# A decoder layer's last token tile: work rows and banks of its own, its merge in four parts, its steps reordered

## Chip, cores and metric

One core of one Trainium2 chip. The metric is the device time of one execution of the whole kernel in microseconds, median of several runs. All arithmetic on the path discussed here is float32, apart from the bf16 operands of the quantized matmuls.

## The reference, cut to what matters

Eight sequences of 128 tokens with 256 features go through three blocks, each followed by a residual addition and a layer norm: a selective state-space scan, a cross attention with 16 heads over 128 context rows, and a feed-forward block with Hadamard transforms and quantization. The change touches the end of the second block and the third:

```
x = layernorm(x + scan_block(x))
x = layernorm(x + attention(x, ctx))          # per head: probabilities, context, latent
                                              # ... then ctx @ Wo.T over all heads: the "merge"
h = hbitlinear(x, w_up)                       # fwht(x), 8-bit rounding by the row maximum, matmul
h = square(relu(h))
h = hbitlinear(h, w_down)                     # fwht over 512 columns, rounding, matmul
x = layernorm(x + h)
```

## The kernel before, in words

The scan block runs first (up to some 260 us). Then the attention and the feed-forward block run together, by tiles of 128 tokens: T = 8 tiles, numbered 0 to 7 (T - 2 is tile 6, T - 1 is tile 7). Heads are handled in G = 4 groups of four. A software pipeline written out by hand in `slots`, one version for each engine, interleaves three tiles: projection and attention of tile t, merge and the first steps of tile t - 1, the later steps of tile t - 2. Each engine has its own program, in fixed order, and waits on semaphores that count up by tile or by group; an instruction queued behind a waiting one waits too. Behind the loop stands an epilogue, also by hand, for what is left of tiles 6 and 7 (lines 740 to 755 for TensorE, 1010 to 1022 for ScalarE, 1126 and 1127 for GpSimd, 1427 to 1440 for VectorE).

The functions for one tile:

- `turn_prob`, `context` (TensorE, lines 623 to 642): transposes ("turns") of a group's probabilities into bank 7, and the context matmuls; ScalarE evicts with `take_prob` and `take_ctx` (lines 948 to 958), the latter counts `cte`.
- `merge_heads` (TensorE, line 647): eight accumulating matmuls 128x128 by 128x256, two for each head group, into bank 7 (`merged`). It waits for the evictions of all four groups. A float32 matmul of this size is two records in the trace.
- `norm2` (VectorE, line 1327): residual, layer norm statistics, the power on GpSimd (line 1064), the normalized row, and the two halves of the first Hadamard level (lines 1340 and 1341).
- `ffn(t, step)`: step 5 turns these halves (TensorE) and evicts them (ScalarE); 6 is the Hadamard matmul, then `quantize` of 256 columns on VectorE (lines 1347 to 1358); 7 turns the rounded row; 8 multiplies with the up weights, ScalarE does relu and square (lines 977 and 979); 9 does two Hadamard levels on VectorE (lines 1366 to 1370), turns on TensorE (line 680) and evicts; 10 is the Hadamard matmul and `quantize` of 512 columns; 11 turns (line 690) and evicts (line 982); 12 multiplies with the down weights and adds the residual (line 1382). `norm3` is the last layer norm, then comes a store of the tile.

All steps of all tiles work in one PSUM bank, 6 (`tail`), and in one set of work rows in SBUF (`x2T`, `qf`, `hr`, `hT`, `qb16`, `qT16`, `xh`). That is why step 5 of a tile waits for step 12 of the one ahead:

```python
if step == 5:
    pe.wait_ge(xh_s, t + 1)
    need(pe, ln3, 4 * t - 3)
```

All plain matmuls go through the helper at line 410; turns stand on lines of their own (532, 565, 629, 659, 669, 680, 690). In the epilogue TensorE's order before is: context of group 2, turn of the last group, step 9 of tile 6, context of the last group, step 10 of tile 6, the merge of tile 7, steps 11 and 12 of tile 6, steps 5 to 12 of tile 7. VectorE's is: normalize of the last group, steps 9 and 10 of tile 6, norm2 of tile 7, step 12 and norm3 of tile 6, steps 6, 9, 10, 12 and norm3 of tile 7.

The rope of the attention multiplies in PSUM banks 0 and 1 and writes `pc` and `psn` (1536 words a partition each), which are not used any more once the last group's sum is made, at 487.9 us.

Of the kernel before, what the change touches and what calls it, by code (L numbers as in the profile page):

```python
# [19 lines left out]
BF16 = mybir.dt.bfloat16  # L20
# [4 lines left out]
P = 128  # L25
T = 8
DM = 256
# [4 lines left out]
NH = 16  # L32
# [3 lines left out]
FF = 512  # L36
TOK = T * P
KM = DM // P
# [10 lines left out]
G = 4  # L49
# [15 lines left out]
def need(eng, sem, count):  # L65

    if isinstance(count, int) and count <= 0:
        return
    eng.wait_ge(sem, count)


def decoder_layer(nc, x_fm, x_tiles, wx, wz, conv_w, w_xp, w_dt, b_dt, a_log, d_skip, w_out,
                  w_q, w_kcq, w_qr, w_kr, w_kckv, w_o, ctx_kv, w_up, w_dn,
                  ident_c, rope_q, rope_kv, had, out, zs_dram, ud_dram, x1_dram, a_dram):
    with ExitStack() as stack:
# [6 lines left out]
        ps = stack.enter_context(nc.psum_tensor("ps", [P, 8, 512], F32))  # L82
# [5 lines left out]
        Pw = sb("Pw", [P, NH // 2, DM])  # L88
# [103 lines left out]
        x2T = carve(256).rearrange("p (k n) -> p k n", k=KM)  # L192
# [85 lines left out]
        scores_of = ps[:, 4:6, 0:256].rearrange("p e (i n) -> p e i n", i=2)  # L278
        latent_of = ps[:, 2:4, 0:P]
        context_of = ps[:, 3, 256:512]  # L280
        turned, merged = ps[:, 7, :], ps[:, 7, 0:DM]

        block = stack.enter_context(nc.Block())

# [123 lines left out]
        def _(pe):  # L408
# [232 lines left out]
                                  probT[:, g % 2, 2 * i + e, :])  # L641
                last.then_inc(cxm, 1)

            tail = ps[:, 6, :]
            tail16 = tail.bitcast(BF16)

            def merge_heads(t):
                pe.wait_ge(cte, G * t + G)
                need(pe, ln2, 4 * t - 3)
                for i in range(NH // 2):  # L650
                    last = mm(merged, ctxT[:, i, :], Pw[:, i, :], i == 0, i == NH // 2 - 1)
                last.then_inc(om, 1)

            def ffn(t, step):
                if step == 5:
                    pe.wait_ge(xh_s, t + 1)
                    need(pe, ln3, 4 * t - 3)
                    for k in range(KM):
                        last = pe.transpose(tail[:, k * P:(k + 1) * P], xh[:, k * P:(k + 1) * P], ident[:, :])
                    last.then_inc(t5m, 1)  # L660
                elif step == 6:
                    pe.wait_ge(t5e, t + 1)
                    for k in range(KM):
                        last = mm(tail[:, k * P:(k + 1) * P], x2T[:, k, :], had_s)
                    last.then_inc(t6m, 1)
                elif step == 7:
                    pe.wait_ge(q1_s, t + 1)
                    for k in range(KM):
                        last = pe.transpose(tail16[:, k * P:(k + 1) * P], qb16[:, k * P:(k + 1) * P],
                                            identb[:, :])  # L670
                    last.then_inc(t7m, 1)
                elif step == 8:
                    pe.wait_ge(t7e, t + 1)
                    for k in range(KM):
                        last = mm(tail, qT16[:, k, :], wupq[:, k, :], k == 0, k == KM - 1)
                    last.then_inc(t8m, 1)
                elif step == 9:
                    pe.wait_ge(lev2_s, t + 1)
                    for k in range(FF // P):
                        last = pe.transpose(tail[:, k * P:(k + 1) * P], hr[:, k * P:(k + 1) * P], ident[:, :])  # L680
                    last.then_inc(t9m, 1)
                elif step == 10:
                    pe.wait_ge(t9e, t + 1)
                    for k in range(FF // P):
                        last = mm(tail[:, k * P:(k + 1) * P], hT[:, k, :], had_s)
                    last.then_inc(t10m, 1)
                elif step == 11:
                    pe.wait_ge(q2_s, t + 1)
                    for k in range(FF // P):
                        last = pe.transpose(tail16[:, k * P:(k + 1) * P], qb16[:, k * P:(k + 1) * P],  # L690
                                            identb[:, :])
                    last.then_inc(t11m, 1)
                elif step == 12:
                    pe.wait_ge(t11e, t + 1)
                    for k in range(FF // P):
                        last = mm(tail[:, 0:DM], qT16[:, k, :], wdnq[:, k, :], k == 0, k == FF // P - 1)
                    last.then_inc(t12m, 1)
# [46 lines left out]
            scores(last, T - 1, G - 1)  # L744
            ffn(T - 2, 8)
            context(last - 1, T - 1, G - 2)
            turn_prob(last, T - 1, G - 1)
            ffn(T - 2, 9)
            context(last, T - 1, G - 1)
            ffn(T - 2, 10)  # L750
            merge_heads(T - 1)
            ffn(T - 2, 11)
            ffn(T - 2, 12)
            for step in range(5, 13):
                ffn(T - 1, step)


# [1 line left out]
        def _(act):  # L759
# [197 lines left out]
                act.activation(ctxT[:, 2 * g:2 * g + 2, :].rearrange("p i n -> p (i n)"), context_of,  # L957
                               ACT.Copy).then_inc(cte, 1)

            tail = ps[:, 6, :]  # L960
            tail16 = tail.bitcast(BF16)

            def ffn(t, step):
                if step == 5:
                    act.wait_ge(t5m, t + 1)
                    act.activation(x2T.rearrange("p k n -> p (k n)"), tail[:, 0:256], ACT.Copy).then_inc(t5e, 1)
                elif step == 9:
                    act.wait_ge(t9m, t + 1)
                    act.activation(hT.rearrange("p k n -> p (k n)"), tail, ACT.Copy).then_inc(t9e, 1)
                elif step == 7:  # L970
                    act.wait_ge(t7m, t + 1)
                    act.activation(qT16[:, 0:KM, :].rearrange("p k n -> p (k n)"), tail16[:, 0:256],
                                   ACT.Copy).then_inc(t7e, 1)
                elif step == 8:
                    act.wait_ge(t8m, t + 1)
                    act.wait_ge(deq_s, 2 * t + 1)
                    act.activation(hr, tail, ACT.Relu, scale=deq).then_inc(relu_s, 1)
                    act.wait_ge(relu_s, t + 1)
                    act.activation(hr, hr, ACT.Square).then_inc(sq_s, 1)
                elif step == 11:  # L980
                    act.wait_ge(t11m, t + 1)
                    act.activation(qT16.rearrange("p k n -> p (k n)"), tail16[:, 0:512], ACT.Copy).then_inc(t11e, 1)
# [34 lines left out]
            take_prob(last, G - 1)  # L1017
            ffn(T - 2, 9)
            take_ctx(last, T - 1, G - 1)
            ffn(T - 2, 11)  # L1020
            for step in (5, 7, 8, 9, 11):
                ffn(T - 1, step)


# [106 lines left out]
        def _(dve):  # L1131
# [190 lines left out]
                dve.tensor_tensor(prob[:, g % 2], prob[:, g % 2], rsum.unsqueeze(2).to_broadcast([P, HG, P]),  # L1322
                                  ALU.mult).then_inc(nrm, 1)

            tail = ps[:, 6, :]

            def norm2(t):
                dve.wait_ge(st_x1, 16 * (t + 1))
                dve.wait_ge(om, t + 1)
                need(dve, x3_s, t - 1)  # L1330
                dve.tensor_tensor(xpre2, merged, x1r, ALU.add).then_inc(ln2, 1)
                dve.wait_ge(ln2, 4 * t + 1)
                center(ln2, 4 * t + 1, xpre2, stats2, aggr2, veps2)
                dve.wait_ge(rs2, t + 1)
                need(dve, xr_s, t)
                dve.tensor_scalar(x2_new, xpre2, aggr2[:, 0:1], rstd2, ALU.subtract, ALU.mult).then_inc(x2_s, 1)

                dve.wait_ge(x2_s, t + 1)
                need(dve, t5m, t)
                dve.tensor_tensor(xh[:, 0:P], x2_new[:, 0:P], x2_new[:, P:DM], ALU.add)  # L1340
                dve.tensor_tensor(xh[:, P:DM], x2_new[:, 0:P], x2_new[:, P:DM], ALU.subtract).then_inc(xh_s, 1)

            def quantize(t, n, src, m, inv, de, w, chain, done):


                root = float(np.sqrt(n))
                dve.tensor_reduce(m, src, AX.X, ALU.max, apply_absolute_value=True).then_inc(chain, 1)
                dve.wait_ge(chain, 5 * t + 1)
                dve.tensor_scalar(m, m, Q_EPS * root, 1.0 / QB, ALU.max, ALU.mult).then_inc(chain, 1)
                dve.wait_ge(chain, 5 * t + 2)  # L1350
                dve.reciprocal(inv, m).then_inc(chain, 1)
                dve.tensor_scalar(de, m, 1.0 / root, w, ALU.mult, ALU.mult).then_inc(deq_s, 1)
                dve.wait_ge(chain, 5 * t + 3)
                dve.tensor_scalar(qf[:, 0:n], src, inv, -QB, ALU.mult, ALU.max).then_inc(chain, 1)
                dve.wait_ge(chain, 5 * t + 4)
                dve.tensor_scalar(qf[:, 0:n], qf[:, 0:n], QB, ROUND, ALU.min, ALU.add).then_inc(chain, 1)
                dve.wait_ge(chain, 5 * t + 5)
                dve.tensor_scalar(qb16[:, 0:n], qf[:, 0:n], -ROUND, None, ALU.add).then_inc(done, 1)

            def ffn(t, step, normed=None):  # L1360
                if step == 9:

                    dve.wait_ge(sq_s, t + 1)
# [65 lines left out]
            row_max(last, G - 1)  # L1429
            normalize(last, G - 1)  # L1430
            ffn(T - 2, 9)
            ffn(T - 2, 10)
            norm2(T - 1)
            ffn(T - 2, 12, T)
            norm3(T - 2)
            ffn(T - 1, 6)
            ffn(T - 1, 9)
            ffn(T - 1, 10)
            ffn(T - 1, 12, T)
# [85 lines left out]
```

## Time and profile before

| what | value |
|---|---|
| median of 3 runs | 531.21 us |
| lowest, highest | 529.97, 535.25 us |
| time of the profiled execution | 533.35 us |
| its span | 531.5 us |
| outside the span | 1.85 us |
| mean granted TensorE clock | 0.915 |
| TensorE busy | 430.6 us (81%) |
| VectorE busy | 404.7 us (76%) |
| ScalarE busy | 311.5 us (59%) |
| GpSimd busy | 217.2 us (41%) |

The busy shares are means over stages with different limits, so what a change at the end is worth is read from the last 45 us alone. The granted clock is given as a share of full speed: 1.00 is the level of 2.4 GHz, 0.50 that of 1.2 GHz. Names in the rows are those of the memory regions: `ps` is PSUM, `reg_a` and `reg_b` the large work regions in SBUF (`had_s` lies in `reg_a`, the work rows in `reg_b`), `Pw` the merge's weights, `wupq` and `wdnq` the quantized weights.

### The profile page before, as it was taken

What the parts mean: (1) busy time and instruction counts of PE and PEld (TensorE: products, weight loads), DVE (VectorE), ACT (ScalarE), POOL (GpSimd) and SP (SyncE); (2) the same over time, 40 slices, a digit from 0 to 9 for tenths busy, and PEclk for the clock granted to TensorE, in tenths of its full rate; (3) what the DMA queues carried; (4) which work ended last, traced back from release to release, by engine and by line L of the source; (5) the groups of instructions that cost most, each with busy time, mean ns of one, the idle gap of its engine ahead of it and who ended that gap; (6) DMA issues with size and microseconds to landing.
All of it is one profiled execution on the core that took longest, in us unless ns stands there. A gap on an engine that the chain in (4) does not pass through costs nothing.

```text
span 531.5 us, 10547 instructions
## 1 busy us (share of the span) xinstructions
PE 430.6 (81%) x3616; PEld 345.8 (65%) x3616; DVE 404.7 (76%) x742; ACT 311.5 (59%) x722; POOL 217.2 (41%) x157
## 2 busy tenths in 40 slices
PE   4979923838777586777999999999999999998733
PEld 1435623527667475666888888888888888887512
DVE  1967699978999969996575687877778777876453
ACT  3666996959999969985143444535255453525320
POOL 2300009985987949780323232323233232322010
PEclk9999975978899879967999999999999999999765
DMA  8942633053011511103000000000000000000000
GB/s 295 389 205 81 195 93 108 20 120 110 21 41 30 145 54 51 39 21 123 22 1 2 11 2 22 0 0 20 0 20 0 20 0 0 20 0 20 1 10 10
DMA packets 18652, 30.85 MB, mean 58 GB/s; under 512 B 2112, under 2 KB 11712, under 8 KB 17920
## 3 DMA queue, kind: packets, MB, share of 16 engines
q1 hardware_dynamic: 18624, 30.49, 17.4%
q8 instruction: 16, 0.26, 0.2%
q14 instruction: 12, 0.10, 0.1%
HBM read 24.16 MB, written 6.32 MB: 57 GB/s over the span
## 4 chain that ended last, share of the span: by engine, by line
PE 40%; issue 19%; DVE 19%; ACT 9%; POOL 8%; DMA 3%; SPq 1%; DVEq 1%; POOLq 0%; ACTq 0%
PE ps L410 33%; POOL reg_b L1059 5%; PE ps L532 3%; DVE reg_b L1256 3%; PE ps L629 2%; ACT hc L854 2%; DMA ud_t<-ud_dram 2%; POOL reg_b L1082 2%; DVE ps L1249 2%; DVE ps L1246 2%; DVE reg_b L1309 1%; ACT reg_b L944 1%; ACT ps L846 1%; DVE reg_b L1194 1%; POOL small L1064 1%
## 5 line engine op out<-in xcount | busy, mean ns | idle before, releaser
L1059 POOL TENSOR_TENSOR reg_b<-reg_c,reg_a 128x1024 f32<-128x1024 f32 x56 | 130.4, 2369 | 58.8 <-DVE reg_c L1199 58.6
L1082 POOL TENSOR_TENSOR reg_b<-reg_b 128x768 f32<-128x768 f32 x32 | 58.0, 1811 | 134.5 <-DVE reg_b L1309 107.3
L410 PE MATMUL ps<-x1T,Mw 128*128 (+1 forms) x768 | 95.2, 281 | 0.0
L410 PEld LDWEIGHTS ps<-x1T,Mw 128*128 128x128 f32 x768 | 89.9, 195 | 4.4 <-issue 3.9
L854 ACT ACTIVATE hc<-reg_b,bc 128x512 f32<-128x512 f32 x112 | 80.4, 718 | 20.9 <-PE ps L532 14.7
L532 PE MATMUL ps<-ident,hc 128*128 128x128 f32 x452 | 73.0, 309 | 19.7 <-ACT hc L854 19.3
L1256 DVE SCALAR_TENSOR_TENSOR reg_b<-reg_c,bc,ps 128x512 f32<-128x512 f32 x112 | 81.8, 736 | 0.0
L532 PEld LDWEIGHTS ps<-ident,hc 128*128 128x128 f32 x452 | 58.9, 160 | 30.5 <-ACT hc L854 29.3
L1249 DVE TENSOR_TENSOR ps<-ps,reg_b 128x512 f32<-128x512 f32 x96 | 65.7, 690 | 8.9 <-ACT ps L846 8.8
L846 ACT ACTIVATE ps<-reg_b 128x512 f32<-128x512 f32 x112 | 66.2, 592 | 4.1 <-POOL reg_b L1059 4.1
L944 ACT ACTIVATE reg_b<-ps,small 128x128 f32<-128x128 f32 x128 | 45.1, 367 | 24.5 <-DVE small L1314 24.5
L1064 POOL TENSOR_TENSOR small<-small 128x1 f32<-128x1 f32 x24 | 13.2, 551 | 102.0 <-DVE small L1274 102.0
L938 ACT ACTIVATE reg_b<-ps 128x256 f32<-128x256 f32 x32 | 12.3, 384 | 53.6 <-PE ps L410 53.6
L410 PE MATMUL ps<-reg_b 64*128 64x128 f32 (+1 forms) x512 | 42.6, 294 | 0.7 <-ACT reg_b L938 0.5
L410 PE MATMUL ps<-reg_b,Nw 64*64 64x128 f32 (+1 forms) x768 | 42.0, 287 | 1.2 <-POOL reg_b L1082 1.2
L532 PE MATMUL ps<-ident,ud_t 128*128 128x128 f32 x32 | 7.5, 377 | 39.6 <-DVE yT L1264 17.8
L410 PEld LDWEIGHTS ps<-reg_b,Nw 64*64 64x64 f32 (+1 forms) x768 | 30.4, 150 | 12.7 <-issue 11.6
L410 PEld LDWEIGHTS ps<-reg_b 64*128 64x128 f32 (+1 forms) x512 | 30.4, 162 | 11.4 <-issue 2.6
L410 PE MATMUL ps<-xw,Nw 128*128 128x512 f32 x64 | 29.7, 622 | 7.3 <-DMA xw<-x_fm 7.3
L1308 DVE TENSOR_TENSOR reg_b<-ps,reg_a 128x768 f32<-128x768 f32 x32 | 30.4, 951 | 4.9 <-PE ps L410 4.6
L532 PEld LDWEIGHTS ps<-ident,ud_t 128*128 128x128 f32 x32 | 4.8, 188 | 41.9 <-issue 21.6
L1309 DVE TENSOR_TENSOR reg_b<-ps,reg_a 128x768 f32<-128x768 f32 x32 | 30.3, 947 | 0.0
(143 smaller groups left out, 709.9 us busy)
## 6 DMA issues: line engine op xcount, KB each, us to landing
reg_a<-a_dram SPq DMA_DIRECT2D x4, 1024.0 KB, 7.3
Mw<-w_o SPq DMA_DIRECT2D x1, 2048.0 KB, 15.3
ud_dram<-reg_b SPq DMA_DIRECT2D x4, 512.0 KB, 4.4
zs_dram<-x1T SPq DMA_DIRECT2D x4, 512.0 KB, 3.7
ud_t<-ud_dram SPq DMA_DIRECT2D x8, 256.0 KB, 3.1
zs_t<-zs_dram SPq DMA_DIRECT2D x8, 256.0 KB, 2.6
xw<-x_fm SPq DMA_DIRECT2D x2, 512.0 KB, 6.1
mring<-w_q SPq DMA_DIRECT2D x4, 256.0 KB, 4.1
```

What stands on the lines that cost most here:

```text
L410: return pe.matmul(o, l, r, start=start, stop=stop)
L532: return pe.matmul(o, src, ident[:, :], start=start, stop=stop, is_transpose=True, skip_group_check=True)
L846: act.activation(ps[:, n % RING, :], dA[:, n // SA % RING, n % SA, :], ACT.Exp, scale=-1.0).then_inc(da_s, 1)
L854: act.activation(hc[:, (n + 1) % WRING, :], H[:, n, :], ACT.Copy, scale=bc[:, t, s:s + 1]).then_inc(hc_s, 1)
L944: last = act.activation(prob[:, g % 2, h, :], scores_of[:, h % 2, h // 2, :], ACT.Exp, bias=negm[:, g % 2, h:h + 1], accum_out=sums[:, g % ...
L1059: pool.tensor_tensor(dA[:, g % RING], delta_r[:, bass.ds(t, 1), :].to_broadcast([P, SA, DI]), Abc[:, g * SA:(g + 1) * SA, :], ALU.mult).th ...
L1064: pool.tensor_tensor(r, v, neghalf, ALU.pow).then_inc(o, 1)
L1082: pool.tensor_tensor(rq[:, g % 2].rearrange("p a c n -> p (a c n)"), pc[:, g % 2].rearrange("p a c n -> p (a c n)"), psn[:, g % 2].rearran ...
L1249: dve.tensor_tensor(E_n, E_n, H[:, n, :], ALU.mult).then_inc(dah_s, 1)
L1256: dve.scalar_tensor_tensor(H[:, n, :], step_du(t), step_b(t, n), ps[:, n % RING, :], ALU.mult, ALU.add).then_inc(h_s, 1)
L1308: dve.tensor_tensor(pc[:, g % 2], v, ropeq_s[:, 0], ALU.mult)
L1309: dve.tensor_tensor(psn[:, g % 2, ::-1], v, ropeq_s[:, 1], ALU.mult).then_inc(ropem, 1)
```

## The change

The last tile gets its own PSUM banks (0 for the steps, 1 for the merge) and its own work rows, laid over `pc` and `psn`. Its merge is issued as four groups of two matmuls, each behind the eviction of its head group; the first waits also until the last rope has read bank 1. Step 5 of the last tile no longer waits for `ln3` of tile 6. In the epilogue TensorE issues steps 5 and 6 of tile 7 ahead of steps 11 and 12 of tile 6, ScalarE evicts step 5 of tile 7 ahead of step 11 of tile 6, and VectorE does norm2 of tile 7 ahead of step 10's quantize of tile 6, and step 6's quantize of tile 7 ahead of step 12 and norm3 of tile 6. GpSimd's and the DMA queue's programs stay.

```diff
-        turned, merged = ps[:, 7, :], ps[:, 7, 0:DM]
+        turned = ps[:, 7, :]
+        rope_words = pc.rearrange("p b a c n -> p (b a c n)"), psn.rearrange("p b a c n -> p (b a c n)")
+        loop_work = (ps[:, 6, :], ps[:, 7, 0:DM], x2T, qf, hr, hT, qb16, qT16, xh)
+        last_work = (ps[:, 0, :], ps[:, 1, 0:DM], rope_words[0][:, 0:256].rearrange("p (k n) -> p k n", k=KM),
...
+                     rope_words[1][:, 1024:1280])
+
+        def work_of(t):
+
+            return last_work if isinstance(t, int) and t == T - 1 else loop_work
...
+            def merge_group(t, g):
+
+                merged = work_of(t)[1]
+                pe.wait_ge(cte, G * t + g + 1)
+                for i in (2 * g, 2 * g + 1):
+                    last = mm(merged, ctxT[:, i, :], Pw[:, i, :], i == 0, i == NH // 2 - 1)
+                if g == G - 1:
+                    last.then_inc(om, 1)
...
                 if step == 5:
                     pe.wait_ge(xh_s, t + 1)
-                    need(pe, ln3, 4 * t - 3)
+                    if not (isinstance(t, int) and t == T - 1):
+                        need(pe, ln3, 4 * t - 3)
...
             context(last - 1, T - 1, G - 2)
+            pe.wait_ge(ropem, G * T)
+            merge_group(T - 1, 0)
+            merge_group(T - 1, 1)
             turn_prob(last, T - 1, G - 1)
             ffn(T - 2, 9)
+            merge_group(T - 1, 2)
             context(last, T - 1, G - 1)
             ffn(T - 2, 10)
-            merge_heads(T - 1)
+            merge_group(T - 1, 3)
+            ffn(T - 1, 5)
+            ffn(T - 1, 6)
             ffn(T - 2, 11)
             ffn(T - 2, 12)
-            for step in range(5, 13):
+            for step in range(7, 13):
                 ffn(T - 1, step)
...
             take_ctx(last, T - 1, G - 1)
+            ffn(T - 1, 5)
             ffn(T - 2, 11)
-            for step in (5, 7, 8, 9, 11):
+            for step in (7, 8, 9, 11):
                 ffn(T - 1, step)
...
             ffn(T - 2, 9)
+            norm2(T - 1)
             ffn(T - 2, 10)
-            norm2(T - 1)
+            ffn(T - 1, 6)
             ffn(T - 2, 12, T)
             norm3(T - 2)
-            ffn(T - 1, 6)
             ffn(T - 1, 9)
```

## Rows read from the trace of the kernel before

**Rows 1.** The page: the chain's shares by engine, and the granted clock in 40 slices

```profile
PE 40%; issue 19%; DVE 19%; ACT 9%; POOL 8%; DMA 3%; SPq 1%; DVEq 1%; POOLq 0%; ACTq 0%
...
PEclk9999975978899879967999999999999999999765
```

**Rows 2.** The chain that ended last, 485 to 532 us: start us, us, what

```profile
497.66 7.33 PE ps L410 x32
```

**Rows 3.** Timeline 485 to 532 us: start us, us, engine, line, operation, tiles [idle before]

```profile
494.65 0.66 PE L629 MATMUL ps<-ident,reg_b 128*128 128x128 f32 x4 [2.15 <-DVE reg_b L1322]
...
496.54 1.12 PE L680 MATMUL ps<-ident,reg_b 128*128 128x128 f32 x4 [1.23 <-DVE reg_b L1370]
...
497.59 1.12 PE L410 MATMUL ps<-reg_b 128*64 128x128 f32 x8
...
498.64 2.08 PE L410 MATMUL ps<-reg_a,reg_b 128*128 128x128 f32 x8
...
500.51 4.46 PE L410 MATMUL ps<-Pw,reg_b 128*128 128x256 f32 x16
500.75 0.69 DVE L1347 TENSOR_REDUCE small<-ps 128x1 f32<-128x512 f32 x1 [4.27 <-PE ps L410]
...
503.11 0.43 DVE L1358 TENSOR_SCALAR reg_b<-reg_b 128x512 bf16<-128x512 f32 x1
...
505.06 0.42 DVE L1331 TENSOR_TENSOR reg_b<-ps,reg_b 128x256 f32<-128x256 f32 x1 [1.52 <-PE ps L410]
...
507.78 0.28 DVE L1341 TENSOR_TENSOR reg_b<-reg_a 128x128 f32<-128x128 f32 x1
...
510.75 0.42 DVE L1347 TENSOR_REDUCE small<-ps 128x1 f32<-128x256 f32 x1 [0.19 <-PE ps L410]
...
512.44 0.29 DVE L1358 TENSOR_SCALAR reg_b<-reg_b 128x256 bf16<-128x256 f32 x1
...
512.79 0.40 PE L669 MATMUL ps<-identb,reg_b 128*128 128x128 bf16 x2 [2.08 <-DVE reg_b L1358]
...
516.12 0.42 DVE L1366 TENSOR_TENSOR reg_b<-reg_b 128x256 f32<-128x256 f32 x1 [3.38 <-ACT reg_b L979]
...
524.48 0.61 PE L690 MATMUL ps<-identb,reg_b 128*128 128x128 bf16 x4 [2.88 <-DVE reg_b L1358]
525.13 0.60 ACT L982 ACTIVATE reg_b<-ps 128x512 bf16<-128x512 bf16 x1 [5.65 <-PE ps L690]
...
525.78 1.04 PE L410 MATMUL ps<-wdnq,reg_b 128*128 128x256 bf16 x4 [0.69 <-ACT reg_b L982]
```

**Rows 4.** Stretches: sum, busy of PE, PEld, DVE, ACT, POOL, granted clock, DMA

```profile
495.00:496.00 1.00, 0.31 (x3) 0.07 (x1) 0.97 (x3) 0.77 (x2) 0.00 (x0) 0.69 0.00 0
...
502.00:503.00 1.00, 1.00 (x5) 0.83 (x5) 0.97 (x2) 0.00 (x0) 0.00 (x0) 0.90 0.00 0
...
509.00:510.00 1.00, 0.53 (x3) 0.51 (x3) 0.34 (x2) 0.38 (x1) 0.48 (x1) 0.52 0.00 0
```

**Rows 5.** TensorE's timeline one tile earlier, where the granted clock is 1.00

```profile
465.99 0.66 PE L680 MATMUL ps<-ident,reg_b 128*128 128x128 f32 x4
...
468.31 1.06 PE L410 MATMUL ps<-reg_a,reg_b 128*128 128x128 f32 x8
469.30 1.30 PE L410 MATMUL ps<-reg_b 64*128 64x128 f32 x16
...
473.31 3.62 PE L410 MATMUL ps<-Pw,reg_b 128*128 128x256 f32 x16
```

**Rows 6.** The scan: TensorE's timeline, and stretches of line 410 alone (busy, granted clock)

```profile
209.88 0.66 PE L532 MATMUL ps<-ident,ud_t 128*128 128x128 f32 x4 [2.94 <-DVE yT L1264]
...
205.20:208.70 3.50, 1.06 (x8) 1.00 0.00 0
...
222.30:225.70 3.40, 0.00 (x0) 1.00 0.34 96
...
225.70:229.10 3.40, 0.00 (x0) 0.50 0.02 5
```

More of the change, by code:

```diff
@@ L280, in decoder_layer @@
         context_of = ps[:, 3, 256:512]
-        turned, merged = ps[:, 7, :], ps[:, 7, 0:DM]
+        turned = ps[:, 7, :]
+        rope_words = pc.rearrange("p b a c n -> p (b a c n)"), psn.rearrange("p b a c n -> p (b a c n)")
+        loop_work = (ps[:, 6, :], ps[:, 7, 0:DM], x2T, qf, hr, hT, qb16, qT16, xh)
+        last_work = (ps[:, 0, :], ps[:, 1, 0:DM], rope_words[0][:, 0:256].rearrange("p (k n) -> p k n", k=KM),
+                     rope_words[0][:, 256:768], rope_words[0][:, 768:1280],
+                     rope_words[1][:, 0:512].rearrange("p (k n) -> p k n", k=FF // P),
+                     rope_words[1][:, 512:768].bitcast(BF16),
+                     rope_words[1][:, 768:1024].bitcast(BF16).rearrange("p (k n) -> p k n", k=FF // P),
+                     rope_words[1][:, 1024:1280])
+        def work_of(t):
+            return last_work if isinstance(t, int) and t == T - 1 else loop_work
         block = stack.enter_context(nc.Block())
@@ L642, in context @@
                 last.then_inc(cxm, 1)
-            tail = ps[:, 6, :]
-            tail16 = tail.bitcast(BF16)
             def merge_heads(t):
+                merged = work_of(t)[1]
                 pe.wait_ge(cte, G * t + G)
@@ L652, in merge_heads @@
                 last.then_inc(om, 1)
+            def merge_group(t, g):
+                merged = work_of(t)[1]
+                pe.wait_ge(cte, G * t + g + 1)
[3 more added lines that the diff above has]
+                    last.then_inc(om, 1)
             def ffn(t, step):
+                tail, _, x2T, _, hr, hT, qb16, qT16, xh = work_of(t)
+                tail16 = tail.bitcast(BF16)
                 if step == 5:
                     pe.wait_ge(xh_s, t + 1)
-                    need(pe, ln3, 4 * t - 3)
+                    if not (isinstance(t, int) and t == T - 1):
+                        need(pe, ln3, 4 * t - 3)
                     for k in range(KM):
@@ L958, in take_ctx @@
                                ACT.Copy).then_inc(cte, 1)
-            tail = ps[:, 6, :]
-            tail16 = tail.bitcast(BF16)
             def ffn(t, step):
+                tail, _, x2T, _, hr, hT, _, qT16, _ = work_of(t)
+                tail16 = tail.bitcast(BF16)
                 if step == 5:
@@ L1323, in normalize @@
                                   ALU.mult).then_inc(nrm, 1)
-            tail = ps[:, 6, :]
             def norm2(t):
+                merged, xh = work_of(t)[1], work_of(t)[8]
                 dve.wait_ge(st_x1, 16 * (t + 1))
@@ L1343, in quantize @@
             def quantize(t, n, src, m, inv, de, w, chain, done):
+                qf, qb16 = work_of(t)[3], work_of(t)[6]
                 root = float(np.sqrt(n))
@@ L1360, in ffn @@
             def ffn(t, step, normed=None):
+                tail, _, _, qf, hr, _, _, _, _ = work_of(t)
                 if step == 9:
```

## The prediction

> **What bounds the kernel now.** I read the page first, for how much of the kernel is in reach. The chain is 40% TensorE, and the granted clock falls only in the early slices and in the last two or three [rows 1]. The change touches the last 45 us, so I went to the chain of waits of that stretch. Around 500 us it is TensorE alone, 7.33 us of matmuls without a break, up to 504.99 [rows 2]. What those are stands in the timeline: behind step 9 of tile 6 (496.54) come the context of the last head group, step 10 of tile 6, and the whole merge of tile 7, 4.46 us, which ends at 504.97 [rows 3]. Only then does tile 7's second half begin: 505.06 norm2, 508.06 its halves are ready, 510.75 its first quantization, 512.73 done, 512.79 TensorE's step 7; from there to the end of the span (531.5) it is one serial chain of 18.7 us in which engines take turns. So what counts is when step 7 of tile 7 can start.
>
> Two more things are to be seen. TensorE stood idle for 2.15 us, 492.50 to 494.65, waiting for the probabilities of the last group, and again 1.23 us before step 9 [rows 3]. And the clock: granted 1.00 until about 495.3, then 0.50 (the 1.2 GHz level) until about 502.1, full (2.4 GHz) again, and half from 509 to the end [rows 4]. What fell in the low stretch cost nearly double: step 9 took 1.12 us where the same group takes 0.66 a tile earlier, step 10 2.08 against 1.06, and the merge 4.46 against 3.62 [rows 3, 5].
>
> **The change, part by part.**
>
> *Merge in four parts.* The eight matmuls are the same. Parts 0 and 1 need only head groups 0 and 1, long evicted, and bank 1, free since the last rope read. They stand right after the context of group 2, where TensorE idles. At full clock a matmul of the merge takes 3.62/8 = 0.45 us [rows 5], four take 1.81 us, and the hole is 2.15 us: they end at about 494.3, the turn of the probabilities starts at 494.65 as before. Cost nothing; the cover is the wait for VectorE's normalize, and without it (half clock, 0.89 us each) four take 3.6 us and the turn would be 1.4 us late.
>
> *Part 2* (two matmuls, 0.91 us) is queued behind step 9 and ahead of the last context; *part 3* behind step 10. Behind part 3 waits norm2.
>
> *The clock in that stretch.* Filling the hole leaves TensorE pauses of 0.35 and about 1.3 us between 492 and 497 instead of 2.15 and 1.23. Does the clock still fall? A row on each side: ahead of 209.88 TensorE was idle for 2.94 us, after a stretch with 1.06 us of true matmuls, at 1.00; but in 222.3 to 225.7 there were only turns, with shorter pauses, and the next stretch is at 0.50 [rows 6]. With 1.8 us of matmuls put into the hole I take it as held. The Trainium skill has a rule that speaks against it ("TensorE: Matmul & The Clock Gate", Part 4, PE-mode transpose): a transpose does not count as TensorE activity the way a matmul does. The fall behind 222.3 to 225.7 agrees. By that rule 494.3 to 497.2, with nothing but turns and pauses in it, can still bring a fall; that is rival A below.
>
> *Sum to the end of the merge, clock held.* From 496.54 (step 9's start is set by VectorE, unchanged): step 9 0.66, part 2 0.91, context half of the group of 16 (1.30/2 = 0.65), step 10 1.06, part 3 0.91: 4.19 us [rows 5]. Groups overlap at a join (468.31 + 1.06 = 469.37, the next starts at 469.30), so I take off 0.07 twice: 4.05, merge done at 500.59 instead of 504.97. That is 4.38 us earlier: 1.8 from the two parts moved ahead, 2.6 from the clock. The evictions that step 10 and part 3 wait for (0.6 us for 512 columns, as the one at 525.13 [rows 3], less for the context's 256) lie beside part 2 with the context, and beside step 10.
>
> *VectorE's order.* Before, quantize of tile 6 (500.75 to 503.54, 2.79 us) ran while TensorE merged: it was free. Now norm2 stands ahead of it and waits for part 3, so VectorE idles from 496.5 to 500.6 and the 2.79 us stand on the path. In exchange step 12 and norm3 of tile 6, which filled 508.06 to 510.75 ahead of tile 7's quantize, go behind it. Chain: 500.59 + 0.09 to norm2, 3.00 for it (505.06 to 508.06), 503.68; 0.03 + 2.79 for tile 6's quantize, 506.50; 0.03 + 1.98 for tile 7's (510.75 to 512.73), 508.51 [rows 3]. Steps 5 and 6 of tile 7 on TensorE and the eviction between them fitted into those 2.69 us before, part of them at half clock; now they run beside tile 6's quantize (2.79 us), in a bank of their own and without the wait for ln3, and cost nothing. If they didn't fit, it would be by 0.1.
>
> *What is queued on TensorE.* Steps 11 and 12 of tile 6 now stand between step 6 and step 7 of tile 7. They start with tile 6's quantize: 506.50 + 0.05, step 11 0.61, 0.04, eviction 0.60, 0.04, step 12 1.04, at half clock: 508.88 [rows 3]. That is 0.3 us later than tile 7's quantize, and holds step 7 up by so much. (At full clock these two would be up to 0.8 us shorter, half of 1.65, and hidden.) Which level? Before, TensorE's thin stretch from 505 brought half clock by 509 [rows 4]; the new thin stretch starts at 500.6, so I take half. Step 7 of tile 7 then starts at 508.88 instead of 512.79: 3.9 us earlier. Step 12 and norm3 of tile 6 on VectorE end by about 511.5, before tile 7's step 9 can start (3.3 us behind its step 7, as 516.12 stands to 512.79 [rows 3]: 512.2), so they are hidden; so is the store of tile 6, and GpSimd's copy of x2, which is needed only at the last step.
>
> *Own work rows.* Same sizes, same types, the rope buffers' space: 0. Unknown is the price of the added waits (the three on cte and one on ropem, all met long before): between 0 and 0.2 us on TensorE, of which the chain's issue pieces of 0.02 to 0.04 suggest the lower; I take 0. The loop body has the same instructions; 0.
>
> **Sum:** 4.38 - 2.82 (quantize onto the path) + 2.66 (step 12 and norm3 of tile 6, with their gaps, off it: 508.06 to 510.75 is 2.69, less 0.03) - 0.31 (steps 11 and 12) = 3.9 us. The span of this execution goes from 531.5 to 527.6, its own time from 533.35 to 529.45. That execution lies 2.1 us above the median of the runs; against the median of 531.21 the forecast is 527.3.
>
> **Rivals.**
>
> *A: the clock falls all the same (or later, from about 497).* For it: the rule above, and that the place of the fall need not be the same in every execution. Against: the 2.94 us pause that it survived. If everything from 496.54 runs at half clock: 1.12 for step 9, 2 x 0.9 = 1.8 each for parts 2 and 3, 1.05 and 1.87 between the starts of context, step 10 and merge [rows 3], 7.6 us, merge done at 504.2; then 5.9 us to tile 6's quantize and 2.4 us to step 7, 512.5: a gain of only 0.3. With the clock low for about half of it, 2.2. Middle 1.3, 529.9.
>
> *B: more than that.* If the denser TensorE keeps full clock through tile 7's own steps 7 to 12, each is shorter by what the two levels differ by: 9 by 0.46 and 10 by 1.02 [rows 3, 5], 11 and 12 by at most half of their 1.65, 7 and 8, an estimate from these, by 0.5: 2.8 us, and steps 11 and 12 of tile 6 hide too: gain up to 7.0, 524.2. Against: half clock from 509 to the end in the trace before, with the same pauses. For steps 7 and 8 alone, with 0.3 from steps 11 and 12: 4.7, 526.5.
>
> *C: nothing.* The time saved before step 7 comes back, because something else is late (a transfer, x2's copy, the output). Nothing in the profile is near: 531.2.
>
> *D: slower.* The mechanism is VectorE's new order: tile 6's quantize hangs behind part 3. Its point is merge done at 504.5 (512.79 - 2.4 - 5.9): later than that, and the kernel loses. That takes a clock that is low already at 492.4, so that parts 0 and 1 take 3.6 us, hold up the last turn by 1.4, and nothing rises after: context done 492.4, parts 0 and 1 3.6 (496.0), turn and step 9 2.1, then 1.8, 1.05, 1.87 and 1.8 as in A, 504.7: 0.2 slower, and with the waits' upper bound 0.4: 531.6. Against: 1.00 in all rows up to 495.
>
> **How the numbers follow.** Forecast 0.60, A 0.23, B 0.08, C 0.05, D 0.04. About 1% (5.3 us) is what a measurement of this kernel can tell from no change; three runs spread over 5.3 us. The forecast, 0.7%, is inside, and reaches beyond by the runs' spread about 1 time in 6 (0.10); with most of B 0.15 for faster. Slower by over 1% has only that spread behind C and D: 0.02. Within: 0.83. The range takes most of B below (524.9) and A's and part of C's above (530.6), with 0.2 us of waits and the median's own uncertainty in it.
>
> **What would show it.** Right: TensorE busy with Pw matmuls from 492.4 to 494.3; granted clock 1.00 at 496 to 500; L680-like group of 0.66 us at 496.5; merge done near 500.6; norm2 at once; VectorE in the order norm2, quantize of 512, quantize of 256, then tile 6's last step; step 7 of tile 7 near 508.9 behind the wdnq matmuls. Wrong: half clock at 497 to 501 (A); the last turn of probabilities later than 494.7 (D); step 7 long after both of its predecessors; tile 7's steps 9 and 10 at 0.66 and 1.06 (B).

## The result, and the profile after

| | kernel before | changed kernel |
|---|---|---|
| median of 16 runs | 532.5 us | 529.44 us |
| profiled execution, its span | 533.35, 531.5 us | 528.5, 526.7 us |
| mean granted TensorE clock | 0.915 | 0.922 |

The ratio of the two is 0.993, with a 95% interval of 0.9907 to 0.9953: the changed kernel is about 3.7 us faster (the two medians differ by 3.1). One of the 16 runs of the kernel before took 718.59 us and is left out of the ratio as slow; without it the median before is 532.27 us. The forecast was 3.9.

The two profiles can be laid on each other step by step. I measure from the start of step 9's turns of tile 6 (before 496.54, after 495.90). First TensorE's timeline of the changed kernel, 484 to 512 us (columns as in [rows 3]; what was line 410 is line 422 now, 629 is 641, 659 is 681, 669 is 691, 680 is 702, 690 is 712; on VectorE 1331 is 1358, 1347 is 1375, 1358 is 1386, 1382 is 1411):

```profile
488.65 0.93 PE L641 MATMUL ps<-ident,reg_b 128*128 128x128 f32 x4 [0.50 <-DVE reg_b L1350]
...
491.63 0.96 PE L422 MATMUL ps<-reg_b 128*64 128x128 f32 x8
492.52 1.99 PE L422 MATMUL ps<-Pw,reg_b 128*128 128x256 f32 x8
494.35 0.60 PE L641 MATMUL ps<-ident,reg_b 128*128 128x128 f32 x4
495.90 0.66 PE L702 MATMUL ps<-ident,reg_b 128*128 128x128 f32 x4 [0.94 <-DVE reg_b L1399]
496.39 1.03 PE L422 MATMUL ps<-Pw,reg_b 128*128 128x256 f32 x4
497.35 0.66 PE L422 MATMUL ps<-reg_b 128*64 128x128 f32 x8
497.94 1.16 PE L422 MATMUL ps<-reg_a,reg_b 128*128 128x128 f32 x8
498.93 1.03 PE L422 MATMUL ps<-Pw,reg_b 128*128 128x256 f32 x4
503.11 0.69 PE L681 MATMUL ps<-ident,reg_b 128*128 128x128 f32 x2 [3.15 <-DVE reg_b L1368]
...
505.81 0.61 PE L712 MATMUL ps<-identb,reg_b 128*128 128x128 bf16 x4 [0.31 <-DVE reg_b L1386]
507.11 1.03 PE L422 MATMUL ps<-wdnq,reg_b 128*128 128x256 bf16 x4 [0.69 <-ACT reg_b L1009]
507.94 0.42 PE L691 MATMUL ps<-identb,reg_b 128*128 128x128 bf16 x2
```

The Pw matmuls stand in three places: eight records where the pause of 2.15 us was, four behind step 9, four behind step 10, end at 499.96. Step 9 takes 0.66 us and step 10 1.16 (the next group starts 0.99 behind it, as in [rows 5]), where [rows 3] had 1.12 and 2.08. From step 9 to the end of the merge it is 4.06 us, before 8.43. Steps 11 and 12 of tile 6 (lines 712 and the wdnq matmuls) stand right ahead of step 7 of tile 7 at 507.94.

VectorE in the timeline of the changed kernel, same stretch:

```profile
500.05 0.42 DVE L1358 TENSOR_TENSOR reg_b<-ps,reg_b 128x256 f32<-128x256 f32 x1 [4.21 <-issue]
...
502.97 0.68 DVE L1375 TENSOR_REDUCE small<-ps 128x1 f32<-128x512 f32 x1
...
505.66 0.42 DVE L1375 TENSOR_REDUCE small<-ps 128x1 f32<-128x256 f32 x1
...
507.35 0.29 DVE L1386 TENSOR_SCALAR reg_b<-reg_b 128x256 bf16<-128x256 f32 x1
508.18 0.48 DVE L1411 SCALAR_TENSOR_TENSOR reg_b<-ps,small,reg_b 128x256 f32<-128x256 f32 x1 [0.53 <-PE ps L422]
```

VectorE waits 4.21 us for the merge, then does norm2, the quantize of 512 columns (502.97), the quantize of 256 (505.66 to 507.64), and only then tile 6's last add (508.18). Tile 7's step 7 follows its quantize by 0.30 us, where it was 0.06 before, because step 12 of tile 6 is ahead of it on TensorE.

The granted clock in stretches of the changed kernel (columns as in [rows 4]):

```profile
488.00:489.00 1.00, 0.50 (x5) 0.36 (x4) 0.59 (x1) 0.63 (x2) 0.00 (x0) 0.94 0.00 0
492.00:493.00 1.00, 1.00 (x10) 0.80 (x7) 0.00 (x0) 1.00 (x7) 0.00 (x0) 0.85 0.00 0
497.00:498.00 1.00, 1.00 (x11) 0.50 (x10) 0.00 (x0) 0.19 (x1) 0.00 (x0) 1.00 0.00 0
502.00:503.00 1.00, 0.00 (x0) 0.00 (x0) 0.85 (x4) 0.00 (x0) 0.08 (x1) 0.77 0.00 0
```

It was full from about 492.3 to 502.5, so over the whole packed stretch, and half again from there to the end. But it had been half from 488.9 to 492.3, ahead of the changed steps, which it was not before. The edits don't reach that stretch: three of the kernels below (the parts alone, VectorE's order turned back, the merge earlier still) have the same program up to there, and their granted clock was 1.00 all through it. Of the variants below one alone shows the early fall too, that with TensorE kept busy in the last chain, and it has the same program up to there.

The span adds up. At tile 6's first quantize the changed kernel was 1.43 us ahead (485.81 against 487.24). That is not the edit's doing as far as the profiles tell: the same instruction starts between 484.46 and 489.29 in the profiles of the experiments. The half clock at 489 to 492 took 0.79 of it (the turn at 488.65 took 0.93 us instead of 0.66, and what follows it was longer likewise). The changed steps gave 16.25 - 12.04 = 4.21 us from step 9 of tile 6 to step 7 of tile 7. The rest, step 7 to the end of the span, is 18.76 against 18.71. 1.43 - 0.79 + 4.21 - 0.05 = 4.8 us, which is 531.5 - 526.7. So these two spans differ by more than the runs do on average, and only the 4.21 is the change's own.

### The profile page after: what moved, and what is told of

Read it like the earlier page. It is cut to its first block and busy times, and to the rows that moved or that the text cites. A ratio compares the mean times of both kernels' runs of the same rounds, so it can differ in the third digit from the quotient of the medians.

```text
span 526.7 us, 10546 instructions
## 1 busy us (share of the span) xinstructions
PE 428.1 (81%) x3616; PEld 342.2 (65%) x3616; DVE 404.5 (77%) x742; ACT 311.6 (59%) x722; POOL 217.2 (41%) x157
## 5 line engine op out<-in xcount | busy, mean ns | idle before, releaser
L422 PE MATMUL ps<-x1T,Mw 128*128 (+1 forms) x768 | 93.7, 279 | 0.0
L422 PEld LDWEIGHTS ps<-x1T,Mw 128*128 128x128 f32 x768 | 88.4, 192 | 4.4 <-issue 3.9
```

The source lines that it names most:

```text
L422: return pe.matmul(o, l, r, start=start, stop=stop)
```

## The experiments

Medians and ratios are against runs of the kernel before on the same chip, with the 95% interval of the ratio. "Step 7" is the start of step 7 of tile 7 counted from the start of step 9's turns of tile 6, in the one profile of each kernel. The times tell most variants from the kernel before, but not from each other: the interval of the changed kernel (0.9907 to 0.9953) overlaps those of nearly all of them. What one variant gives over another is read from their profiles.

The runs go by names: split_only is the parts alone, order_only everything but the early merge, banks_only the own banks and rows alone, fill_mm and fill_turns the pause filled with matmuls or turns, norm_late VectorE's order turned back, merge_early the merge earlier still, warm TensorE kept busy in the last chain, early_warm the last two together, and early_warm_all the same with small fillers.

### The merge in four parts alone

```diff
-        last_work = (ps[:, 0, :], ps[:, 1, 0:DM], rope_words[0][:, 0:256]...
+        last_work = (ps[:, 6, :], ps[:, 1, 0:DM], x2T, qf, hr, hT, qb16, qT16, xh)
...
             merge_group(T - 1, 3)
-            ffn(T - 1, 5)
-            ffn(T - 1, 6)
             ffn(T - 2, 11)
```

(and TensorE's, ScalarE's and VectorE's order and the wait for ln3 as before)

> Only the merge in four parts, into bank 1; steps, work rows, the wait for ln3 and the order of VectorE and ScalarE as before. I measure from the start of tile 6's step 9 turns to the start of tile 7's step 7 (before 16.25 us, changed kernel 12.04). Mine (two gains, merge off the path with the clock held, and the order): merge done 4.05 us behind the step 9 turns as in the changed kernel, quantize of tile 6 ends at 6.0, norm2 at 9.05, then step 12 and norm3 of tile 6 2.7 and tile 7's quantize 2.0: step 7 at 13.8, so 2.4 us of the 4.2. Rival (banks, rows and order bring it): 16.2. Rival (the parts bring all of it): 12.0.

530.45 us against 533.39, ratio 0.9952 (0.9926 to 0.9978). Timeline of TensorE:

```profile
494.38 0.66 PE L696 MATMUL ps<-ident,reg_b 128*128 128x128 f32 x4 [1.24 <-DVE reg_b L1390]
...
497.41 1.03 PE L417 MATMUL ps<-Pw,reg_b 128*128 128x256 f32 x4
...
508.30 0.39 PE L685 MATMUL ps<-identb,reg_b 128*128 128x128 bf16 x2 [2.08 <-DVE reg_b L1377]
```

Merge done at 498.44, 4.06 us behind step 9, exactly as in the changed kernel; step 7 at 13.92 (expected 13.8). So the parts bring 2.3 of the 4.2 us (the times alone, 0.9952 against 0.993, don't resolve this). Here norm2 starts at 500.32, 1.9 us after the merge, since tile 6's quantize stands ahead of it.

### Everything but the early merge

```diff
-            merge_group(T - 1, 0)
-            merge_group(T - 1, 1)
             turn_prob(last, T - 1, G - 1)
             ffn(T - 2, 9)
-            merge_group(T - 1, 2)
             context(last, T - 1, G - 1)
             ffn(T - 2, 10)
-            merge_group(T - 1, 3)
+            for g in range(G):
+                merge_group(T - 1, g)
```

> The changed kernel with all four parts of the merge together behind step 10 of tile 6; banks, rows and orders as in the changed kernel. Mine: the pause of 2.15 us is open again, the clock falls, merge done about 8.4 us behind the step 9 turns; then 0.1 + 3.0 + 2.75 + 1.95 and steps 11 and 12: step 7 at 16.3 to 16.6 us, the same as before or 0.3 slower (with the clock held by chance 5.8 and 13.8). Rival (order and own banks bring the gain): 12 to 14 with the clock low.

532.6 us against 533.39, ratio 0.9997 (0.9968 to 1.0026): nothing. Timeline and stretches:

```profile
496.65 0.66 PE L702 MATMUL ps<-ident,reg_b 128*128 128x128 f32 x4 [1.22 <-DVE reg_b L1397]
...
499.86 4.19 PE L422 MATMUL ps<-Pw,reg_b 128*128 128x256 f32 x16
...
512.02 0.42 PE L691 MATMUL ps<-identb,reg_b 128*128 128x128 bf16 x2
```

```profile
497.00:498.00 1.00, 1.00 (x12) 0.50 (x10) 0.00 (x0) 0.60 (x1) 0.00 (x0) 0.79 0.06 16
500.00:501.00 1.00, 1.00 (x4) 0.82 (x3) 0.00 (x0) 0.00 (x0) 0.00 (x0) 0.50 0.00 0
501.00:502.00 1.00, 1.00 (x6) 0.87 (x6) 0.00 (x0) 0.00 (x0) 0.00 (x0) 1.00 0.00 0
```

With the pause open the clock fell again, but later, at about 497.6, and was back at 501.0. So the merge was done 7.40 us behind step 9 (I had expected 8.4), and step 7 came at 15.37. The number that tells about the order doesn't depend on that: from the end of the merge to step 7 it is 7.97 us, before 7.82, changed kernel 7.98. The new order behind a late merge is 0.15 us longer, not shorter.

### Own banks and rows alone

The edit keeps the changed kernel's banks and rows and does without the wait for ln3, with `merge_heads(T - 1)` whole and all orders as before.

> The own banks, the own work rows and the step 5 without the wait for ln3 alone: merge whole, all orders as in the kernel before. Mine: step 5 of tile 7 may start at once behind norm2 (0.5 us earlier, beside step 12's add), but VectorE is in norm3 of tile 6 until its quantize anyway: step 7 of tile 7 at 16.1 us behind the step 9 turns instead of 16.25 (with a clock fallen later, up to 1.7 less for both): gain 0.15, not measurable in the time. Rival (the single bank was what held tile 7 up): gain above 1 us.

533.35 us against 533.62, ratio 1.0003 (0.9977 to 1.003). Timeline of TensorE:

```profile
493.77 1.11 PE L702 MATMUL ps<-ident,reg_b 128*128 128x128 f32 x4 [1.24 <-DVE reg_b L1393]
...
497.74 4.38 PE L422 MATMUL ps<-Pw,reg_b 128*128 128x256 f32 x16
...
509.67 0.40 PE L691 MATMUL ps<-identb,reg_b 128*128 128x128 bf16 x2 [2.26 <-DVE reg_b L1380]
```

Step 7 at 15.90 us (493.77 to 509.67), from the end of the merge 7.55 against 7.82: 0.27 us in the profile where I expected 0.15, nothing in the time. Most of the 0.27 is VectorE's wait of 0.19 us for step 6 of tile 7 (at 510.75 in [rows 3]), which is gone here. The single bank was not what held tile 7 up.

### The clock alone: the pause filled, the merge where it was

```diff
             context(last - 1, T - 1, G - 2)
+            pe.wait_ge(ropem, G * T)
+            pe.wait_ge(cte, G * (T - 1) + 2)
+            for i in range(4):
+                mm(ps[:, 1, 0:DM], ctxT[:, i, :], Pw[:, i, :], i == 0, i == 3)
             turn_prob(last, T - 1, G - 1)
```

> The kernel before, with four extra matmuls 128x128 by 128x256 into the free bank 1 in the pause before the last turn of probabilities; their result is not used, the merge is made whole afterwards as before. Tells what the clock alone is worth. Mine: granted clock stays 1.00 through the merge, merge done 5.85 us behind the step 9 turns instead of 8.43, step 7 at 13.7 instead of 16.25. Rival (the clock falls by other things than this pause): 16.2, half clock at 496 to 502.

530.8 us against 533.39, ratio 0.9954 (0.9927 to 0.998): four matmuls more, and the kernel is faster. In the profile:

```profile
494.81 0.66 PE L680 MATMUL ps<-ident,reg_b 128*128 128x128 f32 x4 [1.23 <-DVE reg_b L1374]
495.39 0.66 PE L410 MATMUL ps<-reg_b 128*64 128x128 f32 x8
496.15 1.16 PE L410 MATMUL ps<-reg_a,reg_b 128*128 128x128 f32 x8
497.14 3.62 PE L410 MATMUL ps<-Pw,reg_b 128*128 128x256 f32 x16
...
504.40 0.66 PE L659 MATMUL ps<-ident,reg_b 128*128 128x128 f32 x2 [2.12 <-DVE reg_b L1386]
```

Step 9 and the merge have their full-clock durations of [rows 5], and step 10 is 0.99 from start to start as there; the merge is done at 500.76, 5.95 us behind step 9 (expected 5.85). Step 7 came at 14.03, expected 13.7: 0.1 is the merge, the rest is that the clock now fell at 503.8, ahead of steps 5 and 6 of tile 7, which at half clock (0.66 and 1.22 us) ran 0.44 us past norm3, where it was 0.19 before.

Set beside the parts alone (step 7 at 13.92), this tells something the sum did not: the clock alone gives 2.2 of their 2.3 us. That half of the merge is moved out of the way ends it 1.9 us sooner, but behind VectorE's old order that is worth only 0.1 us at step 7.

The same with turns in place of the matmuls (`pe.transpose(ps[:, 1, ...], ctxT[:, i % 4, :], ident[:, :])`, twelve of them):

> As fill_mm, but the pause is filled with 12 turns of 128x128 (about 1.8 us too) instead of four matmuls. If a turn does not count as activity (the rule of the Trainium skill, TensorE: Matmul & The Clock Gate, Part 4): clock falls as before, step 7 at 16.2 behind the step 9 turns. If only pauses count: as fill_mm, 13.7. I lean to the rule, 60 to 40.

531.25 us against 533.39, ratio 0.9959 (0.9933 to 0.9985): the same gain. Timeline and stretches:

```profile
490.41 1.53 PE L750 MATMUL ps<-ident,reg_b 128*128 128x128 f32 x12
492.62 0.66 PE L629 MATMUL ps<-ident,reg_b 128*128 128x128 f32 x4 [0.68 <-DVE reg_b L1326]
494.52 0.66 PE L680 MATMUL ps<-ident,reg_b 128*128 128x128 f32 x4 [1.24 <-DVE reg_b L1374]
```

```profile
490.00:493.00 3.00, 2.32 (x23) 1.91 (x22) 1.06 (x4) 2.84 (x11) 0.00 (x0) 1.00 0.02 5
493.00:496.00 3.00, 1.66 (x16) 1.01 (x15) 1.43 (x4) 1.53 (x4) 0.00 (x0) 1.00 0.00 0
496.00:499.00 3.00, 3.00 (x18) 2.76 (x19) 1.84 (x6) 0.19 (x1) 0.00 (x0) 1.00 0.00 0
```

From 490.5 to 495.1 TensorE did nothing but turns, with pauses, and the clock stayed at 1.00. My lean to the rule was wrong. The rule, that a transpose does not count as a matmul does (Trainium skill, "TensorE: Matmul & The Clock Gate", Part 4, PE-mode transpose), isn't borne out by these float32 turns.

The trace of the kernel before had a stretch that spoke against it too, and that the prediction left out beside 222.3 to 225.7 (sum, TensorE busy, granted clock, DMA):

```profile
239.40:242.80 3.40, 2.11 (x18) 1.00 0.10 34
```

Line 410 has nothing in it, so these 2.11 us are turns alone, and the next 3.4 us are at 1.00 as well. Why the clock fell behind 222.3 to 225.7 (1.34 us of turns) isn't shown.

### VectorE's order turned back

```diff
             ffn(T - 2, 9)
-            norm2(T - 1)
             ffn(T - 2, 10)
+            norm2(T - 1)
             ffn(T - 1, 6)
```

> The changed kernel with VectorE doing tile 6's quantize (step 10) ahead of norm2 of tile 7, as in the kernel before; all else changed. Tests whether the order that I charged 2.82 us for is right in its place. Mine: quantize runs 3.1 to 5.9 us behind the step 9 turns, norm2 5.95 to 8.95, then steps 5 and 6 of tile 7 stand bare on the path (half clock 2.4 us), tile 7's quantize to 13.4, step 7 at 13.45 instead of 12.04: 1.4 us slower than the changed kernel, with the clock held there 0.9. Rival (norm2's wait for the merge costs; the old order is better): 11.5 to 12.

530.96 us against 533.64, ratio 0.9958 (0.9931 to 0.9985). Step 7 at 13.44 (497.40 to 510.84), as expected to 0.01 us, 1.4 us later than in the changed kernel. What the quantize costs in front of norm2 stands here, from the last instruction of norm2 to tile 7's quantize:

```profile
506.05 0.28 DVE L1368 TENSOR_TENSOR reg_b<-reg_a 128x128 f32<-128x128 f32 x1
508.80 0.42 DVE L1375 TENSOR_REDUCE small<-ps 128x1 f32<-128x256 f32 x1 [2.47 <-PE ps L422]
```

VectorE stands idle for 2.47 us while TensorE and ScalarE do steps 5 and 6. In the changed kernel tile 6's quantize fills that.

### The merge earlier still

```diff
             turn_prob(last, T - 1, G - 1)
-            ffn(T - 2, 9)
             merge_group(T - 1, 2)
             context(last, T - 1, G - 1)
-            ffn(T - 2, 10)
+            ffn(T - 2, 9)
             merge_group(T - 1, 3)
+            ffn(T - 2, 10)
```

(ScalarE evicts the last context ahead of step 9's turns)

> The changed kernel with TensorE in another order: part 2 of the merge right behind the last turn of probabilities, the last context ahead of step 9 of tile 6, part 3 between steps 9 and 10 (it stood behind 10); ScalarE evicts the last context ahead of step 9. Measured from the start of VectorE's step 9 of tile 6 (changed kernel: merge done 5.67 us later, step 7 of tile 7 at 13.65). Mine: the merge sets the path, merge done at 3.7, step 7 at 11.7, 1.95 us faster than the changed kernel, some 5.6 faster than before. Rival (step 10's quantize becomes the path, or evictions hold part 3): gain under 0.5.

527.89 us against 533.64, ratio 0.9882 (0.9844 to 0.9919). Timeline:

```profile
496.99 0.43 DVE L1395 TENSOR_TENSOR reg_b<-reg_b 128x256 f32<-128x256 f32 x1 [0.34 <-ACT reg_b L1006]
...
499.48 1.13 PE L422 MATMUL ps<-Pw,reg_b 128*128 128x256 f32 x4
500.45 1.05 PE L422 MATMUL ps<-reg_a,reg_b 128*128 128x128 f32 x8
...
508.59 0.42 PE L691 MATMUL ps<-identb,reg_b 128*128 128x128 bf16 x2
```

Merge done 3.62 us and step 7 11.60 us behind the start of VectorE's step 9, against 5.67 and 13.65 in the changed kernel: 2.05 us, expected 1.95. The end of the merge sets the path, one for one.

### TensorE kept busy in the last chain

```diff
+            def keep_warm(n):
+                for i in range(n):
+                    mm(ps[:, 5, 0:DM], ctxT[:, i % 8, :], Pw[:, i % 8, :], i == 0, i == n - 1)
...
             merge_group(T - 1, 3)
+            keep_warm(5)
             ffn(T - 1, 5)
...
             for step in range(7, 13):
                 ffn(T - 1, step)
+                if step in (8, 10):
+                    keep_warm(5)
```

> The changed kernel with five extra matmuls 128x128 by 128x256 into the free bank 5 (result not used) in each of three pauses of TensorE: ahead of step 5, behind step 8 and behind step 10 of tile 7. Measures my case B: what half clock costs on the last chain. From the start of tile 7's step 7 to the end of the span: before 18.7, changed 18.8. Mine, if the pauses are what lowers the clock: granted 1.00 to the end, 16.1 us, 2.6 faster. Rival (the clock falls all the same): five matmuls take 4.5 us at half clock in pauses of 3.0, 21 to 22 us, slower than the changed kernel by some 3.

527.73 us against 533.64, ratio 0.9872 (0.9828 to 0.9916). Neither side was right in the profile: step 7 to the end of the span took 17.3 us, 1.5 less than in the changed kernel. The clock was half from about 508 to 514.9 and full behind it:

```profile
512.00:513.00 1.00, 1.00 (x4) 0.82 (x3) 0.46 (x1) 0.97 (x2) 0.39 (x2) 0.50 0.00 0
514.00:515.00 1.00, 1.00 (x4) 0.82 (x3) 0.60 (x2) 0.00 (x0) 0.00 (x0) 0.56 0.01 1
518.00:519.00 1.00, 1.00 (x6) 0.88 (x5) 0.93 (x5) 0.00 (x0) 0.00 (x0) 1.00 0.00 0
```

Five matmuls, most of them at half clock (4.04 us, from 511.42), held the turns of step 9 up by some 0.6 us (they started at 515.30, VectorE was done at 514.61). Steps 9 to 12 behind them, at full clock, more than won it back.

> merge_early and warm together. Mine: both gains add, some 4.5 us less than the changed kernel, about 8 less than before (ratio 0.985). Rival: with the merge done earlier the pause ahead of step 5 meets the extra matmuls otherwise and one of the two gains is lost: ratio 0.990 or above.

Together: 524.54 us against 533.64, ratio 0.9849 (0.9806 to 0.9891). The gains add within the intervals: 0.8% below the changed kernel, where the two alone were 0.5 and 0.6. In the profile it is 16.8 us from step 7 (505.94) to the end, with half clock at 505.3 to 508.7. With small fillers in the short pauses as well (against early_warm):

```diff
+            pe.wait_ge(ropem, G * T)
+            for i in range(2):
+                mm(ps[:, 1, 0:DM], ctxT[:, i, :], Pw[:, i, :], i == 0, i == 1)
             to_latent(last, G - 1)
...
             ffn(T - 1, 6)
+            keep_warm(2)
             ffn(T - 2, 11)
+            keep_warm(1)
             ffn(T - 2, 12)
             for step in range(7, 13):
                 ffn(T - 1, step)
-                if step in (8, 10):
-                    keep_warm(5)
+                if step < 12:
+                    keep_warm(5 if step in (8, 10) else 1)
```

> early_warm with small fillers too: two matmuls into bank 1 ahead of the last latent group, two behind step 6 of tile 7, one behind step 11 of tile 6 and one behind each of steps 7, 9 and 11 of tile 7. In early_warm the granted clock was 0.50 from 505.3 to 508.6 and again from 519. Mine: 1.00 from 484 us to the end, step 7 of tile 7 to the end of the span 16.1 us (early_warm 16.8), less 0.1 to 0.2 for each filler that hangs over: some 0.3 us better than early_warm at best. Rival: the fillers hold up the steps behind them (0.45 us each in pauses of 0.5 to 0.7, double at half clock): 17 us or more, slower than early_warm.

523.35 us against 533.62, ratio 0.9794 (0.9767 to 0.9822), the best of all: 10 us less than before. Its interval overlaps that of early_warm, so what the small fillers add is seen in the profile alone. Stretches of its profile:

```profile
505.00:506.00 1.00, 0.80 (x6) 0.31 (x4) 0.94 (x4) 0.51 (x1) 0.00 (x0) 1.00 0.00 0
512.00:513.00 1.00, 0.89 (x8) 0.89 (x9) 0.00 (x0) 0.06 (x1) 0.00 (x0) 1.00 0.00 0
519.00:520.00 1.00, 0.00 (x0) 0.00 (x0) 0.31 (x2) 0.00 (x0) 0.55 (x1) 0.63 0.00 0
```

Full clock until 519.3, when only the last layer norm is left; step 7 to the end 16.24 us (16.1 expected), 2.5 less than in the changed kernel.

## Why the prediction was right

**The part that carries it, the merge.** Forecast 4.05 us from step 9 to the end of the merge with the clock held; measured 4.06, in the changed kernel and in the run with the parts alone. That it fits to 0.01 is in part luck: from start to start step 9 took 0.49 us where the sum has 0.66, part 2 took 0.96 and part 3 1.03 where it has 0.91 each, and the errors cancel. The clock held, as taken. It was at 1.00 from the last turn of probabilities to the end of the merge in all nine profiles in which the pause is filled, by matmuls or turns, and it fell in the three in which it is open (before, order_only, banks_only). The clock's share was put at 2.6 us of the 4.38: with the pause filled and nothing else changed, the merge was done 8.43 - 5.95 = 2.5 us earlier.

**VectorE's order.** Forecast: 2.82 us of quantize onto the path, 2.66 us of step 12 and norm3 off it. Measured: norm2 at 500.05 to 503.05, then quantizes to 505.75 and 507.64, each some 0.1 us sooner than my sum, since the next reduction starts before the last write of the one ahead has ended. With the merge late, the order gives nothing (0.9997; 7.97 against 7.82 us from the merge to step 7). What the forecast's sum hides is that it depends on the merge: with the merge early and the old order, norm2 waits 1.9 us for tile 6's quantize, and step 7 is at 13.92 instead of 12.04. So the two edits give 2.3 and 0 apart (the second costs 0.15) and 4.2 together.

**Steps 11 and 12 in the way of step 7.** Forecast: step 7 0.37 us behind VectorE's last write instead of 0.06, so 0.31 later, at half clock. Measured: 0.30 behind it, so 0.24 later. With matmuls in the pauses it was 0.06 as before (early_warm, 505.88 to 505.94).

**Cost nothing:** the added waits, own rows and banks (1.0003). The waits are not seen in the sum of 4.06.

**The sum** was 12.34 us from step 9 to step 7; it came out as 12.04. Of the 0.3, 0.24 is the overlap of VectorE's instructions at two joins, and 0.07 steps 11 and 12. In the time the forecast was 3.9 us less, and the ratio says 3.7 (2.5 to 5.0). The median itself, 529.44 us, lies 2.1 above the 527.3 that was forecast: 1.3 of it because the three runs that the forecast started from had a median of 531.21, and all 16 have 532.5. The profile of before that I summed from was one in which the clock was low from 495.3 to 502.1 (merge done at 8.43). The forecast took that for every execution. In the run of banks and rows alone it was much the same (8.35), but in that of the order alone the fall came later and the low stretch lasted 3.4 us (7.40). The gain therefore differs by about 1 us from one execution to the next, and an average lies under that of my profile. That this explains the difference of 0.2 us isn't shown; it is far inside the interval.

**The rivals.** A (the clock falls all the same in the changed kernel) was not seen in its profile, nor in those of the other kernels that fill the pause. Whether it happens in other executions stays open. One reason I gave for it, the rule about turns, wasn't borne out by fill_turns. B (full clock to the end) doesn't come by itself, half clock came at 502.5; but forced by fillers it is worth 2.5 us, forecast 2.8. C is out. D's first half nearly happened: the clock was half until 492.3, and parts 0 and 1 began at 492.52. Made late by the slow steps ahead of them, they held the last turn back by 0.35 us (it started at 494.35 without a pause, with its input ready by 494.0). That cost nothing, since the last context waits behind step 9 anyway, and the parts themselves ran at full clock. My evidence against D, full clock in all rows up to 495, was one execution's.

## What to carry to other kernels

Work that is pulled ahead into a pause of TensorE can pay twice: once for itself, and once because the matmuls behind it run at full clock. Here the second was the larger, 2.5 against 1.9 us at the end of the merge, and it can be had alone by matmuls or turns whose result nobody uses. The first reached the end of the kernel only with VectorE's new order. When a sum has two edits in it, ask of each what it gives without the other: VectorE's new order, with the own banks, was worth 1.9 us behind an early merge and nothing behind a late one. And look where the end of such a merge could go further: an order one step bolder gave another 2 us in the profile, one for one.

## What the runs showed of the hardware

The place at which the clock falls isn't tied to the program. With the pause open it fell 1.2 us ahead of step 9's turns (495.3, the kernel before), at about the same place in banks_only (492.4, 1.3 us ahead), and 0.9 us behind them in order_only (497.6). With one and the same program up to there, it fell at 488.9 in the changed kernel's profile and not at all in those of split_only, norm_late and merge_early. The low stretch lasted 3.4 us (changed kernel, order_only) or 6.8 us (before, banks_only). A single profile of a stretch with pauses should be read with that in mind. Twelve turns of float32 in the pause kept the clock at 1.00 as four matmuls did, with nothing but turns from 490.5 to 495.1. Extra matmuls at the wrong level cost: five took 4.04 us, most of it at half clock, where 2.32 is their full-clock time (both in warm).
